# Ternary FFN weights spilled as int8 through casting DMAs on the GpSimd queue, and two fences per attention group

## What is computed

```python
def weight_quant(w):
    scale = 1.0 / jnp.clip(jnp.mean(jnp.abs(w)), EPS)
    wq = jnp.clip(jnp.round(w * scale), -1.0, 1.0) / scale
...
def bitlinear(x, w):
    return jnp.einsum('bsh,oh->bso', act_quant(x), weight_quant(w))
...
gate = bitlinear(x, w_gate)                # 2048 -> 8192
up = bitlinear(x, w_up)                    # 2048 -> 8192
return h_bitlinear(silu(gate) * up, w_down)   # Hadamard transform, then 8192 -> 2048
```

## Time and profile before

| | us |
|---|---|
| Median of two runs (8988.89 and 9025.4) | 9007.15 |
| The profiled execution, device time | 8931.42 |
| Span of its slowest core (core 2) | 8929.9 |
| Shortest span among its cores (core 4) | 8850.5 |

### The profile page before, as it was taken

How to read it: one execution, slowest core, us unless ns; L and a number is a source line. 1 busy time by engine, 2 the same in 40 slices (tenths; PEclk the granted TensorE clock), 3 DMA queues, 4 the chain that set the end, 5 groups by cost and what they waited for, 6 DMA issues and landing times. The chain is left out here.

```text
span 8929.9 us, 80349 instructions; the slowest of 8 cores (8850.5 to 8929.9 us)
## 1 busy us (share of the span) xinstructions
PE 4413.7 (49%) x31046; PEld 2680.8 (30%) x31174; DVE 3999.9 (45%) x3071; ACT 212.5 (2%) x271; POOL 0.2 (0%) x4
## 2 busy tenths in 40 slices
PE   7747364534645463624490144443144915925925
PEld 1113121234412121324430122222023814814814
DVE  0133333343344434243437755557855183183184
ACT  0000000000000000000010000000000000000000
POOL 0000000000000000000000000000000000000000
PEclk9968676755676786855595555656566958967967
DMA  7622424320252434230034277772277805805805
GB/s 243 210 77 71 148 75 144 110 83 21 63 175 72 142 83 149 76 131 30 25 114 141 72 186 190 194 191 71 71 217 220 264 1 182 278 12 175 276 21 170
DMA packets 992610, 1154.74 MB, mean 129 GB/s; under 512 B 110314, under 2 KB 798699, under 8 KB 966635
## 3 DMA queue, kind: packets, MB, share of 16 engines
q1 hardware_dynamic: 992236, 1149.60, 43.5%
HBM read 1006.83 MB, written 142.66 MB: 129 GB/s over the span
## 5 line engine op out<-in xcount | busy, mean ns | idle before, releaser
L621 PE MATMUL pbk<-BA 128*128 128x512 bf16 x4512 | 1201.1, 435 | 1169.7 <-DVE BA L569 1169.2
L1371 PE MATMUL pbk<-BA 128*128 128x256 bf16 x5120 | 815.9, 331 | 768.4 <-DVE BA L1329 738.1
L621 PEld LDWEIGHTS pbk<-BA 128*128 128x128 bf16 x4608 | 498.1, 109 | 1846.5 <-issue 1522.5
L1371 PEld LDWEIGHTS pbk<-BA 128*128 128x128 bf16 x5120 | 583.5, 116 | 989.4 <-issue 834.4
L1568 PE MATMUL pbk<-BA 128*128 128x256 bf16 x2560 | 388.1, 320 | 789.4 <-DVE BA L1535 396.1
L450 DVE TENSOR_REDUCE redp<-AR 128x1 f32<-128x2048 f32 x192 | 438.9, 2286 | 356.5 <-DMA AR<-wgT 126.7
L1568 PEld LDWEIGHTS pbk<-BA 128*128 128x128 bf16 x2560 | 281.8, 113 | 895.6 <-issue 828.2
L709 PE MATMUL pbk<-BA 32*32 32x32 bf16 x6144 | 344.9, 223 | 412.4 <-PEq L666 412.4
L709 PEld LDWEIGHTS pbk<-BA 32*32 32x32 bf16 x6144 | 344.2, 145 | 414.6 <-issue 414.6
L1371 PE MATMUL pbk<-BA,TB 128*128 128x256 bf16 x3072 | 364.6, 277 | 21.5 <-DMA TB<-tG 13.5
L280 PE MATMUL pbk<-AR,cfm 128*1 128x512 f32 x768 | 338.4, 600 | 53.7 <-DMA AR<-wmod 52.7
(11 more groups left out here) (183 smaller groups left out, 4138.9 us busy)
## 6 DMA issues: line engine op xcount, KB each, us to landing
AR<-wgT SPq DMA_DIRECT2D x128, 1024.0 KB, 9.7
AR<-wuT SPq DMA_DIRECT2D x128, 1024.0 KB, 9.7
AR<-wdT SPq DMA_DIRECT2D x128, 1024.0 KB, 7.3
AR<-wmod SPq DMA_DIRECT2D x24, 4096.0 KB, 16.3
BA<-tG SPq DMA_DIRECT2D x96, 512.0 KB, 4.8
BA<-tU SPq DMA_DIRECT2D x96, 512.0 KB, 4.9
TB<-tG SPq DMA_DIRECT2D x96, 512.0 KB
TB<-tU SPq DMA_DIRECT2D x96, 512.0 KB, 5.0
```

The lines of the kernel that those rows point to most:

```text
L621: mm = t.matmul(bank[:, :], wof[:, ci * 128:(ci + 1) * 128], mv[:, ci * 512:(ci + 1) * 512], start=first, stop=(wof is wsL and ci == 15))
L1371: mm = t.matmul(bank[:, slot * QT:slot * QT + QT], tsrc[:, ci * 128:(ci + 1) * 128], h2q_all[:, ci * 1024 + q4 * QT:ci * 1024 + q4 * QT + QT],
```

## The change

The three scratch tensors become int8. The spill of a ternary tile (bf16 in the core's memory, int8 in HBM) and its reload (int8 in HBM, bf16 in the core's memory) therefore change the type on the way. All of them, 192 spills and 576 reloads, move from SP's queue to GpSimd's, on a pool of their own, `PG`, with 6 semaphores. SP keeps the fp32 weight loads, x2 and y. What each transfer waits for stays as it was. In the core's memory a tile is still bf16, with the same buffers and the same matmuls.

Apart from that, `emit_group` no longer carries its two finer waits from one group to the next; it begins with a `fence()`, and has a second one ahead of the block with the square.

```diff
-    tG = nc.dram_tensor("tG", [128, 64 * 2048], BF16, kind="Internal").ap()
+    tG = nc.dram_tensor("tG", [128, 64 * 2048], I8, kind="Internal").ap()
...
+    PG = DPool("pg", 6)
...
     def emit_group(half, g):
+        fence()
...
-                w0 = [(sDV.h, grp_state['tr_dv'])] if grp_state['tr_dv'] is not None else []
-                toks.append(PL.load(q, vG, vscr[:, g * 2048:(g + 1) * 2048], waits=w0))
+                toks.append(PL.load(q, vG, vscr[:, g * 2048:(g + 1) * 2048]))
...
+        fence()
         with nc.Block() as blk:
             @blk.scalar
             def _(s):
-                s.wait_ge(sDV.h, sDV.v)
                 s.activation(AMsq, AM, AF.Square).then_inc(sAC.h, 1); sAC.v += 1
...
+            @blk.gpsimd
+            def _(g):
+                for j in range(128):
+                    oc, which = j // 2, j % 2
                     scr = tG if which == 0 else tU
                     if q4 == 0:
...
-                        if j >= 1:
-                            jj = j - 1
-                            sc2 = tG if jj % 2 == 0 else tU
-                            spl_toks[jj] = PL.load(
-                                q, sc2[:, (jj // 2) * 2048:(jj // 2 + 1) * 2048],
-                                bav(tern_of(jj), 2048), waits=[(sDV.h, tern_dv[jj])])
+                        spl_toks[j] = PG.load(
+                            g, scr[:, oc * 2048:(oc + 1) * 2048],
+                            bav(tern_of(j), 2048), waits=[(sDV.h, tern_dv[j])])
...
-                        ld_toks.append(PL.load(
-                            q, tbuf4(j),
+                        ld_toks.append(PG.load(
+                            g, tbuf4(j),
                             scr[:, oc * 2048:(oc + 1) * 2048], waits=waits))
```

More of the change, by code:

```diff
@@ L174, in fence @@
         vals = ([(s.h, s.v) for s in (sPE, sDV, sAC) if s.v > 0]
-                + [(h, v) for (h, v) in PL.toks() + PO.toks() if v > 0])
+                + [(h, v) for (h, v) in PL.toks() + PO.toks() + PG.toks() if v > 0])
         with nc.Block() as blk:
@@ L689, in _ @@
                 sDV.v += 1
-                grp_state['tr_dv'] = sDV.v
         dv_min = sDV.v
@@ L1271, in _ @@
             def _(q):
+                if q4 != 0:
+                    return
                 for j in range(128):
@@ L1274, in _ @@
                     wsrcT = wgT if which == 0 else wuT
+                    waits = [(sDV.h, tern_dv[j - 2])] if j >= 2 else []
+                    ld_toks.append(PL.load(
+                        q, f32v(AR4, 8192 + which * 2048, 2048).rearrange(
+                            "p (ci f) -> p ci f", f=128),
+                        wsrcT[:, oc * 128:(oc + 1) * 128].rearrange(
+                            "(ci p) f -> p ci f", p=128),
+                        waits=waits))
+            @blk.gpsimd
+            def _(g):
+                for j in range(128):
+                    oc, which = j // 2, j % 2
                     scr = tG if which == 0 else tU
                     if q4 == 0:
[L1277 to L1289 removed]
+                        spl_toks[j] = PG.load(
+                            g, scr[:, oc * 2048:(oc + 1) * 2048],
+                            bav(tern_of(j), 2048), waits=[(sDV.h, tern_dv[j])])
                     else:
@@ L1491, in _ @@
                                 waits=waits))
[L1492 to L1502, removed]
                     if fo >= 1:
@@ L1514, in _ @@
                     qt2[:, 0:QT], waits=[(sDV.h, ev_dv[15])])
+            @blk.gpsimd
+            def _(g):
+                for j in range(64):
+                    fo, sub = j // 4, j % 4
+                    if q4 == 0:
+                        spl_toks[j] = PG.load(
+                            g, tD[:, j * 2048:(j + 1) * 2048],
+                            bav(tern_of(j), 2048), waits=[(sDV.h, tern_dv[j])])
+                    else:
+                        waits = ([(sPE.h, pe_b + j - 3)] if j >= 4
+                                 else [(sPE.h, gup_pe_end - 4 + j + 1)])
+                        ld_toks.append(PG.load(
+                            g, tbuf4(j),
+                            tD[:, j * 2048:(j + 1) * 2048], waits=waits))
             @blk.vector
```

20 lines of the change are left out of this document (3 added, 17 removed).

## The result

The changed kernel takes 8792.33 us, median of 11 runs (8733.67 to 8917.53); the kernel before, run on the same chip, takes 8993.69 us (10 runs, 8908.54 to 9098.73). The ratio is 0.9793, with a 95% interval of 0.9742 to 0.9844: faster by 1.6 to 2.6%. In some executions, of either kernel, the four cores of one die run at a lower granted clock and take one or two per cent longer; the medians in us count all runs, the ratios leave these out. The forecast was 9430 us, and its range began at 8860, 68 us above what came. The profiled execution after took 8807.0 us, against 8931.42 before.

The account below looks back on a forecast made before the run. No engine bounds the whole: gate/up reloads run near TensorE's rate, down reloads are DMA-bound, first-quarter VectorE waits for fp32 loads. Reloads 330 + starts 12 + first quarter 60 + fences 23 = +425 on 9007, said as 9430 us; range 8860 to 10000.

Parts of the forecast that it names:

- The price of a converted row: Weight-block spills and reloads: a type-changing DMA costs 2.5 us a tile, bounds 1.16 and 2.99, break-even about 1.95.
- Reloads: Six later gate/up and down blocks: dearer converted rows add 213 us in gate/up and 117 in down, together +330.
- First quarter: First gate/up and down blocks: dearer spills +77, loads freed and fewer HBM writes -17, so +60 us, bounds -163 and +173.
- Starts: First loads of each of six reload blocks: slower rows and software queue add 2 us each, +12 us (0 to +20).
- Fences: Attention groups: 16 new fences at 1.47 us each, +23 us (bounds 0 and +30).
- The range: Whole kernel: 9120 to 9840 us within the likeliest case, the dearer row; 8860 to 10000 overall.
- Relief of HBM: Rival, weight blocks: conversion is free and TensorE bounds the reloads; 8870 us, 8747 at the first quarter's bound; chance 0.36.
- GpSimd's issue as the bound: Rival, reload blocks: GpSimd needs over 1.95 us per DMA and sets the pace; at 4 us, 10200 us; chance 0.10.
- The late spill: Rival, first quarter: held-up GpSimd issue lands spills after the next conversion needs them; 9330 us at 3 us late; chance 0.06.

## Why the prediction was wrong

**The price of a converted row** is the step that failed, and with it the sign. I took 2.5 us a tile, from bounds of 1.16 and 2.99, because the 8 KB fp32 row seemed the nearest relative; measured, it is 1.61. DMAs of the window 7330 to 7455 after, a down block of reloads:

```profile
q0 software_dynamic: 8943, 32.59, 79.9%
q1 hardware_dynamic: 4320, 3.93, 9.5%
```

79.9% of 16 engines for 125 us is 1598 us for 32.59 MB: 49.0 us per MB, 0.201 us for a row of 4,096 bytes, 1.61 us a tile. Before it was 52.3 and 0.214. In the trace's records of single rows, the median converted reload row took 175 ns and the plain one 159, so the conversion costs 16 ns. The tail gives back more: in the six reload blocks, over all eight cores, the slowest twentieth begins at 333 ns after and 474 before, the slowest hundredth at 595 and 1021, and the mean falls from 202 ns to 195. A tile has landed when its slowest row has, so this fits the landing of 3.5 us in place of 4.8; it is read from the two traces and not tested by itself. The fp32 scratch measured what an 8 KB side costs, 3.3 us a tile; it was the wrong relative. My argument against the rival, "half the bytes are only half on one side of the transfer", was true and had no weight, if that side is the crowded one.

**Reloads**, forecast +330, measured -62. Beside the price, the reading under it was wrong: I called the blocks bound by the DMA engines at a share of 0.83 to 0.89, and wrote that "the ring of four buffers doesn't shorten this". For gate/up the ring was the bound. With bf16 rows and six buffers the blocks took 228 us at a share of 0.90. With four, the plain rows on GpSimd have a cycle 0.42 us longer than on SP (0.2 landing, 0.22 issue), 0.42 / 4 x 128 = 13 us, and 15 to 18 were seen. After the change the landing is 1.3 us shorter and the issue 0.22 longer, (0.54 + 3.5 + 1.83) / 4 = 1.47 us, well under PE's 1.745, and -12, -9, -12 were seen, most of what was to be had down to 228. The cycle is an estimate by medians; that the ring and not the engines held the block at 246 rests on the run with six buffers. In down, the change made -11, -10, -9. Plain rows came there only with both, more buffers and GpSimd's queue: the queue alone 146 to 149 us, the ring alone 133 to 138, both 123 to 126.

**First quarter**, forecast +60 with bounds of -163 and +173, measured -124. The queue and the order do nothing there that shows in the total (two runs at a ratio of 0.999 and 1.000). Half the bytes by themselves give -78 and -33, together -111. So the term had its sign from the price of the row, and its bound of -163 from the load's way being cleared, which gave nothing. The spill did become late, as one rival said, but not from GpSimd, and it cost nothing: with room for four tiles the wait for it went and the loads took its time.

**Starts**, forecast +12: PE waits 7.19, 6.13 and 7.40 us for the first gate/up tile of a quarter, where it waited 5.91, 6.89 and 7.51, and the three down blocks begin with the same idle time of 117 to 118 us in the median of the cores: nothing. **Fences**, forecast +23, measured +22: right, and worked from the right rows. **The range** was added up wrongly too: with 2.2 us a tile and the other terms at their lower bounds the sum is 9007 + 159 - 163 = 9003, not 9120. Even that is 211 us above what came.

**The rivals.** Relief of HBM, given 0.36 with only 0.10 for faster, is what happened; its time of 8870, or 8747 at the first quarter's bound, stands on both sides of 8792. Its sizes were the wrong way round: I gave the reloads -132 and they made -62, and the first quarter -40 where it made -124. The windows alone could not have told: 0.77 of 16 engines at 190 GB/s is 65 us of engine time per MB in the first quarter, against 49 in the reloads at 0.83 and 270, but most of this is the length of the rows, 27 ns for 512 bytes (53 us per MB) against 159 for 4,096 (39). It is in the tails of the rows that relief shows. GpSimd's issue as the bound, with a limit of 1.95 us for a DMA, is refuted by 0.54. The late spill: the Trainium skill (SBUF — State Buffer, section Who interferes with whom) has VectorE, in its two-port modes, shut GpSimd out of a shared port pair, so that it can't write descriptors. The groups after allow a little of that, 593 and 771 ns for the spills of tG and tD against 538 for a reload, and 532 for tU. That is 0.2 us, not the microseconds by which the landing moved; the same lateness came from SP.

What stays open: that other cores crowd HBM is my reading of the tail of row times, and no run with fewer cores was made. The equal times of pairs of cores in the first block suggest that what is crowded is shared by two cores and not by all eight; that isn't shown either. How the gain of bytes splits between reads and writes in the first quarter is not known either.

## What to carry to other kernels

A DMA engine share of 0.83 beside an idle consumer doesn't say that the engines are the bound: work out the cycle of one buffer (issue, landing, use) over the number of buffers, and compare it with the consumer's pace first. Where many cores stream from HBM, price a transfer by the bytes on each side separately, and price the conversion by the side that is longer; here the narrow scratch was worth its conversion. And when reloads share an in-order queue with stores that wait for an evacuation, put them on another queue, even one that issues more slowly.

## What the hardware showed that I had not expected

- A DMA that converts int8 to bf16 takes 175 ns for a row of 4,096 bytes in the median, against 159 without a conversion; fp32 to bf16 costs 413 ns in the mean, with 8,192 bytes on the longer side.
- A spill of 256 KB lands later (8.9 us) than one of 512 KB did (6.2), because it now starts beside a 1 MB load; moved in the same way, one of 512 KB took 10.8.
- In the first quarter, loads and spills pace each other: a third load buffer alone gives nothing (953 us, in the execution at a low clock), two more ternary buffers alone nothing (966), both together 85 us of 935.
- GpSimd issues a DMA of 128 rows in 0.54 us with or without conversion (0.77 to 0.79 in the mean for the spills of tD), against SP's 0.32.
- In the first gate/up block cores 4 and 5 took the same time to 0.4 us and cores 6 and 7 to 0.3 us, while the two pairs lay 66 us apart.
